# Marks of the chosen cells moved to ScalarE, the low digit's one-hot in one comparison, and new orders, in an audio tower kernel

## The reference, cut to what matters

```
sc0, ix0 = top_k(s0, 16); sc1, ix1 = top_k(s1, 16)      # 64 keys each
cs = sc0[:, None] + sc1[None, :]                         # 16 x 16 cells
ci = ix0[:, None] + ix1[None, :]                         # the expert of a cell
fs, pos = top_k(cs, 16); fi = ci[pos]
w = softmax(fs)
inner = einsum(h, expert_down[fi]); act = gelu(inner)
out = sum over heads and chosen experts of (act * w) @ expert_up[fi]
```

## Time and profile before

| | us |
|---|---|
| median of 3 runs | 1461.08 |
| lowest and highest | 1459.81, 1461.68 |
| profiled execution | 1458.15 |
| its span, first to last instruction | 1456.3 |
| VectorE busy | 1332.5 (91%) |
| TensorE busy | 1219.2 (84%) |
| GpSimd busy | 975.1 (67%) |
| ScalarE busy | 894.5 (61%) |

### The profile page before, as it was taken

How to read it: one execution, slowest core, us unless ns; L and a number is a source line. 1 busy time by engine, 2 the same in 40 slices (tenths; PEclk the granted TensorE clock), 3 DMA queues, 4 the chain that set the end, 5 groups by cost and what they waited for, 6 DMA issues and landing times.

```text
span 1456.3 us, 41234 instructions
## 1 busy us (share of the span) xinstructions
PE 1219.2 (84%) x9633; PEld 711.9 (49%) x9633; DVE 1332.5 (91%) x10235; ACT 894.5 (61%) x4105; POOL 975.1 (67%) x1850
## 2 busy tenths in 40 slices
PE   4788887898888988888887979898898889998873
PEld 2434554644554464545445445554645555463343
DVE  4349999999999999999999999999999999998995
ACT  2566757567576656757675775767567576655532
POOL 4428667686867668586766857577685867667562
PEclk7777687767777676877867786687668777675655
DMA  2000000000000000000000000000000000000000
GB/s 52 12 6 2 3 10 4 4 8 5 9 4 10 3 5 10 5 9 4 11 4 4 10 4 10 5 10 4 5 8 6 4 4 5 3 4 3 5 3 7
DMA packets 22351, 10.49 MB, mean 7 GB/s; under 512 B 13839, under 2 KB 21951, under 8 KB 22080
## 3 DMA queue, kind: packets, MB, share of 16 engines
q1 hardware_dynamic: 21456, 7.30, 2.1%
q10 hardware_dynamic: 624, 0.30, 0.1%
HBM read 4.58 MB, written 3.01 MB: 5 GB/s over the span
## 4 chain that ended last, share of the span: by engine, by line
DVE 35%; PE 28%; issue 15%; POOL 14%; ACT 7%; SPq 1%; POOLq 1%; DVEq 0%; DMA 0%; ACTq 0%
DVE idx L1404 8%; DVE val L1402 5%; DVE oh L1417 4%; DVE scores L1407 4%; DVE cr L1471 4%; PE bankS L1132 3%; PE bankS L1131 3%; PE bankQ L1121 3%; PE bankQ L1120 3%; DVE best L1469 3%; ACT ns_junk L829 3%; PE bankM L1168 3%; PE bankQ L1108 2%; POOL std L561 2%; DVE wl L1436 2%
## 5 line engine op out<-in xcount | busy, mean ns | idle before, releaser
L1404 DVE FIND_INDEX8 idx<-val,scores 124x8 uint16<-124x64 f32 x1536 | 304.8, 217 | 0.0
L1168 PE MATMUL bankM<-wl,oh 128*128 128x16 f16 x5952 | 163.7, 173 | 59.5 <-DVE wl L1436 59.5
L1402 DVE MAX8 val<-scores 124x8 f32<-124x64 f32 x1536 | 211.1, 209 | 2.1 <-ACT scores L836 2.0
L1168 PEld LDWEIGHTS bankM<-wl,oh 128*128 128x128 f16 x5952 | 161.2, 101 | 72.6 <-issue 41.1
L595 POOL TENSOR_TENSOR ce<-idxf 124x128 f32<-124x128 f32 (+4 forms) x240 | 95.4, 429 | 115.9 <-ACT idxf L843 115.8
L829 ACT ACTIVATE ns_junk<-bankQ 124x32 f32<-124x32 f32 x768 | 138.2, 265 | 37.7 <-PE bankQ L1121 37.7
L1417 DVE TENSOR_SCALAR oh<-eh 128x992 f16<-128x992 int16 x384 | 150.4, 457 | 2.3 <-ACT eh L877 2.3
L1407 DVE MATCH_REPLACE8 scores<-val,scores 124x64 f32<-124x64 f32 x768 | 151.7, 208 | 0.0
L569 POOL TENSOR_TENSOR qscale<-nmx,power 124x16 f32<-124x16 f32 x48 | 139.9, 2914 | 0.0
L829 ACT ACTIVATION_READ_ACCUMULATOR ns_junk<-bankQ 124x1 f32 x768 | 138.3, 278 | 0.0
L1132 PE MATMUL bankS<-bias9k,std9T 9*124 9x512 f32 x192 | 132.2, 774 | 0.0
(11 more groups left out here) (188 smaller groups left out, 3185.0 us busy)
## 6 DMA issues: line engine op xcount, KB each, us to landing
x_in<-in_x SPq DMA_DIRECT2D x16, 93.8 KB
x_in<-in_x SPq DMA_DIRECT2D x16, 62.5 KB
out<-o_sb SPq DMA_DIRECT2D x16, 62.0 KB
out<-o_sb SPq DMA_DIRECT2D x16, 61.0 KB
out<-o_sb SPq DMA_DIRECT2D x16, 60.5 KB
x_in<-in_x SPq DMA_DIRECT2D x16, 31.0 KB
conv_w<-in_L_tok_kernel ACTq DMA_DIRECT2D x2, 128.0 KB, 3.0
fwq_in<-in_L_ffn_Wq SPq DMA_DIRECT2D x1, 256.0 KB
```

The source lines that it names most:

```text
L1168: last = e.matmul(coef[:, g, :, :], oh[:, k, g, :, :].rearrange("p v t -> p (v t)"), wl[:, part, k, :, TG * g:TG * (g + 1)], start=k + par ...
L1402: last = v.max(out=v_[:, hd, s, best8], in_=src[:, hd, s, :])
L1404: last = v.max_index(out=i_[:, hd, s, best8], in_max=v_[:, hd, s, best8], in_values=src[:, hd, s, :])
```

## The change

Three things. First, the filler becomes a power of two, `taken` becomes f16, and `mark` leaves VectorE: ScalarE copies `cr` with the scale 4096 / filler, which gives 4096 where the filler stands and rounds to 0 elsewhere. Its semaphore is `marked`. VectorE's first replacement of the next tile waits for it, since it overwrites `cr`. `chosen` counts 10 per tile. Second, a constant tile `lows` holds 0, 1, 2, 3, and `one_low` compares the whole with it in one instruction. Third, the orders of all engines but SyncE are written anew.

```diff
-NEG = -1.0e30
+NEG = -2.0 ** 100
...
-        taken = sb("taken", [NT, H, NC])
+        taken = sb("taken", [NT, H, NC], f16)
...
+        lows = sb("lows", [128, EL, NT], i16)
...
# GpSimd, select
-                pool.wait_ge(chosen, 11 * n + 9)
+                pool.wait_ge(marked, n + 1)
...
# ScalarE
+            def mark(c, t):
+
+                n = c.tile(t)
+                act.wait_ge(chosen, 10 * n + 8)
+                wait(act, weights, 4 * n - 2)
+                a.activation(taken[:, :, :], cr[:, :, :], ACT.Copy, scale=WSCALE / NEG).then_inc(marked, 1)
...
# VectorE
+                for l in range(EL):
+                    v.memset(lows[:, l, :], l)
...
-                for l in range(EL):
-                    last = v.tensor_scalar(ol[:, :, l, :], el[:, :, :], float(l), None, ALU.is_equal)
-                last.then_inc(wl_ready, 1)
+                v.tensor_tensor(ol[:, :, :, :], el[:, :, :].unsqueeze(2).to_broadcast([128, 2, EL, NT]),
+                                lows[:, :, :].unsqueeze(1).to_broadcast([128, 2, EL, NT]), ALU.is_equal).then_inc(wl_ready, 1)
...
+                    if step == 1 and q == 0:
+                        wait(dve, marked, n)
...
-            def mark(c, t):
-
-                n = c.tile(t)
-                wait(dve, weights, 4 * n)
-                dve.wait_ge(chosen, 11 * n + 8)
-                v.tensor_scalar(taken[:, :, :], cr[:, :, :], NEG / 2, WSCALE, ALU.is_lt, ALU.mult).then_inc(chosen, 1)
```

More of the change, by code:

```diff
@@ L292, in build @@
         chosen = sem("chosen")
+        marked = sem("marked")
         weights = sem("weights")
@@ L579, in rank_sums @@
                     pool.wait_ge(ranked, 16 * n + 6)
-                    wait(pool, chosen, 11 * n - 7)
+                    wait(pool, chosen, 10 * n - 6)
                     wait(pool, exp_ready, n)
@@ L649, in body @@
                 do(p1_rstd, c + 2, 0)
+                do(q_scale, c, 2)
+                do(select, c, 1)
+                do(normalise, c, 1)
+                do(rank_sums, c, 2, 0)
+                do(rank_sums, c, 2, 1)
+                do(rank_sums, c, 2, 2)
                 if at(c, -2):
@@ L883, in body @@
             def body(c):
[L884 to L887, removed]
+                do(weight_high, c + -1, 2)
                 do(q_squares, c, 1)
                 do(p1_probs, c + 1, 1)
-                do(weight_high, c + -1, 2)
                 do(p1_attnT, c + 1, 0)
                 do(p1_diag, c + 1, 1)
+                do(q_stdT, c, 1)
                 do(cells_T, c + -1, 2)
                 do(p1_axT, c + 1, 0)
-                do(q_stdT, c, 1)
                 do(p1_probs, c + 1, 2)
+                do(merged_weights, c + -1, 2)
+                do(p1_attnT, c + 1, 1)
                 do(index_floats, c, 0)
-                do(p1_attnT, c + 1, 1)
-                do(merged_weights, c + -1, 2)
                 do(p1_diag, c + 1, 2)
@@ L903, in body @@
                 do(cell_exp, c, 0)
+                do(q_scores, c, 1)
                 do(best_exps, c, 0)
-                do(q_scores, c, 1)
+                do(mark, c, 0)
                 do(p1_axT, c + 1, 1)
@@ L929, in body @@
                     copy_weights()
+                do(q_stdT, c + 1, 0)
+                do(mark, c, 1)
+                do(p1_ln, c + 2, 0)
                 do(cell_exp, c, 1)
-                do(q_stdT, c + 1, 0)
-                do(p1_ln, c + 2, 0)
                 do(q_norms, c + 1, 0)
@@ L938, in body @@
                 do(q_gelu, c + 1, 1)
+                do(cells_T, c, 1)
                 if at(c, -1):
                     q_scores(c + 1, 0)
-                do(cells_T, c, 1)
                 do(q_gelu, c + 1, 2)
+                do(index_floats, c, 2)
                 do(merged_weights, c, 1)
                 do(q_gelu, c + 1, 3)
+                do(cell_exp, c, 2)
                 do(p1_probs, c + 2, 0)
-                do(index_floats, c, 2)
+                do(mark, c, 2)
                 do(best_exps, c, 2)
+                do(p1_diag, c + 2, 0)
+                if not at(c + 1, 0):
+                    do(q_scores, c + 1, 0)
             run(act, start, body, lambda: None)
@@ L1180, in body @@
             def body(c):
+                do(scatter, c + -2, 1)
+                do(p1_scores, c, 2)
                 do(turn_cells, c + -2, 2)
@@ L1587, in body @@
                 do(choose, c, 0, 1)
-                do(choose, c, 0, 2)
                 do(one_high, c + -1, 2, 0)
```

90 lines of the change are left out of this document (41 added, 49 removed).

## The result

The changed kernel takes 1474.54 us (median; 1466.17 to 1488.98) against 1459.81 us of the kernel before (1448.09 to 1465.1), 11 runs each on the same chip: a ratio of 1.012, 95% interval 1.0089 to 1.0152. The execution of 1488.98 us is a slow one and is left out of the ratio; the next is 1485.58. It is slower by 1.2%, where 1.5% faster was forecast, and lies above the range. The profiled execution took 1481.37 us with a span of 1479.6, 23.3 us more than the span before. It is 6.8 us over the median, at a mean granted clock of 0.694 of full speed; the kernel before was profiled at 0.723.

A forecast was written before the change was run, and what follows sets the result against it. VectorE, busy 97.3% of the steady stretch, was taken as the bound. Savings of 13.4 + 11.0 = 24.4 us, 23.4 after head and tail, less 2 for handing over, gave 21.4 off 1461.08: 1439.5 us, range 1428 to 1458.5.

The forecast's parts named there:

- I take 0 for it, bounds -10 and +10: New step orders on the engines: no time won or lost, within 10 us either way.
- Sum. 13.4 + 11.0: VectorE time saved by moving the marks (13.4 us) and by the single low-digit comparison (11.0 us), added to 24.4 us.
- one microsecond less of VectorE work per batch is close to one microsecond less per batch: Steady stretch: VectorE work saved becomes nearly equal time saved, as long as the other engines follow.
- 13 disturbed ones, 1.1 us each: Low-digit one-hot on VectorE: the single comparison gains 1.1 us in each of 13 tiles disturbed by GpSimd's `sq_pairs` and `sq_win`.
- `wl` never over 781 ns: VectorE's two-input product `wl`, sometimes beside GpSimd's work, peaked at 781 ns; evidence against the new comparison being held up.
- The marks leave VectorE: 48 `taken` instructions leave VectorE, 0.28 us each from start to start: 13.4 us of VectorE time go.
- their arrival on ScalarE: 48 mark copies on ScalarE, 27 us, hidden by its free time; handing over to `select` loses 2 us, bounds 0 and 12.
- The slower rival: Tile 0's mark holds `axT` and `attnT` on ScalarE, `res` on VectorE waits; 2.4 us per batch gives 1475 us; chance 0.10.
- The first rival: Another engine, TensorE by its clock or ScalarE, takes up half of the gain: 1450 us; chance 0.13.
- The rival of a comparison held up beside the window sums: New comparison delayed 1.2 us at a time beside `sq_pairs` and `sq_win`, a loss of 4.6 us: 1454.5 us; chance 0.07.
- The signs: Observations set to show the forecast wrong: `ol` above 1 us, `res` waits above 15 us, VectorE under 95%, `oh` above 480 ns.
- the rival at one column per cycle: New low-digit comparison runs as slowly as f32 tensor-tensors, losing 10.8 us: 1458.5 us; chance 0.05.

The follow-up runs named there:

- scores first: Kernel before with marks on ScalarE, which copies tile 1's scores before tile 0's `best_exps` and `mark`: 1447.08 us; with the one comparison too 1464.72 us.
- run 5: Marks with scores first, both halves of tile 2's `oh` moved ahead of `choose` and the low digit: 1442.55 us with four comparisons, 1461.14 with one.
- run 7: Changed kernel with VectorE's `oh` of tile 1 pulled together ahead of the last two steps of `choose`: 1490.19 us, 1.0222 to the kernel before.
- three pairs: Marks with scores first, four comparisons against one: as is 1447.08 and 1464.72 us, window sums cut 1424.48 and 1440.51, tile 2's `oh` moved 1442.55 and 1461.14.
- the fastest kernel: Fastest complete kernel: marks with scores first, four comparisons, tile 2's `oh` moved ahead of `choose` and the low digit: 1442.55 us, 0.9914 to the kernel before.
- run 3: Changed kernel with GpSimd's order of before, 1473.92 us, or TensorE's order of before, 1474.25 us; ratios to the kernel before 1.0103 and 1.0123.
- run 4: Marks with scores first, GpSimd's window sums cut to 8 to 16 columns: 1424.48 us with four comparisons, 1440.51 us with one.

## Why the prediction was wrong

- **"I take 0 for it, bounds -10 and +10": the orders, the term that failed most.** With the marks and four comparisons they cost 1.8% (0.9935 to 1.0112), with the old instructions 1.8% too (1.0183), some 26 us each. I had bounded them by the idle time of VectorE that they could win and, for the loss, by nothing but symmetry. The row that priced a loss was at hand: an `oh` takes from 414 ns to 1178 ns by what GpSimd does beside it. Four of them beside `select` turned out 1.5 us longer, 21 us in 14 batches, while meetings elsewhere shrank: `oh` as a whole is busy 14.5 us more.
- **"Sum. 13.4 + 11.0": terms priced one by one and added. That step failed too.** The orders have no price of their own. On top of both instructions in the orders of before (1.0176) they take 0.6% away, on top of both with the scores first (1.0056) they add 0.6%, on top of the marks with the scores first 1.8%. And neither does VectorE's time: "one microsecond less of VectorE work per batch is close to one microsecond less per batch" did not hold when the new waits came (run 5: 19.1 us less work, 0.2% less time; run 7: less work and more time).
- **"13 disturbed ones, 1.1 us each": wrong in kind.** The term was right by itself: the slots of `ol`, start to next start, sum to 31.4 us in the changed kernel (31.0 forecast) from 42.5. But the time does not go with the instruction; the GpSimd step delays whatever stands there. An undisturbed one takes 0.59 us by starts against 0.55 for four (0.645 forecast), so nothing was left to gain, and the other direction was missing: the one long comparison holds GpSimd, and in the orders of before one comparison in place of four cost 16 to 19 us in three pairs, none of it without tile 0's. In the new orders that loss does not show (+0.1%), nor does any gain. The evidence that two inputs are safe beside GpSimd, `wl` never over 781 ns, was evidence on the old orders alone: in the changed kernel `wl` takes up to 1266 ns.
- **"The marks leave VectorE", 13.4 us, and their arrival on ScalarE, 2 us: right in mechanism, with one wait overlooked.** With scores first VectorE's busy time falls by 12.7 us and the time by 0.65%, 9.5 us. The steps that I named behind the mark (`axT`, `attnT`) were indeed hidden. In the changed kernel `axT` runs at 710.46, right behind a mark that waited 2.45 us, and TensorE asks for it at 712.78. `q_scores`, which the change moved ahead of the mark and which the prediction does not name, was the wait that mattered: behind the mark it costs 27 us of waiting.
- **The slower rival** gave 1475 us and the result is 1474.5. That is luck: it needed 2.4 us a batch at `res`, 38 us in all, with the gain of 24.4 kept, and `res` waits 18.2 us, 14.5 more than before. Its mechanism, `axT` held behind the mark, is not the cause either: the marks with scores first leave that wait at 4.6 us, and the fastest kernel has 17.7. The first rival, that another engine takes up the gain because of TensorE's clock, was the one that the profile came nearest to, but I let it take half of the gain at most; how far it is the cause stays open (behind run 3). The rival of a comparison held up beside the window sums was right that nothing is saved there.
- **The sums.** 1461.08 less 21.4 is 1439.7, not 1439.5, and the rival at one column per cycle leaves out the 2 us for handing over; with them it is 1460.5. Neither changes the outcome.
- **The signs** that I had set: `oh` above 480 ns came (493 ns). `res` above 15 us in the stretch did not (13.3 us), nor did `ol` above 1 us (0.73 in the mean), nor VectorE under 95% busy (96.0%).
- **What is shown and what is open.** Along one path the runs go -0.65% (marks, scores first), +1.8% (new orders), +0.1% (one comparison, within its interval). That they end at +1.2% is no confirmation, since the last run of the path is the changed kernel. That the new orders, met with the marks, lose what the marks win is shown; by which step is not. The meeting of `select` with tile 1's `oh` is seen in the trace, but removing it (run 7) changed waits as well, and no run held the clock apart from the orders.

## What to carry to other kernels

When VectorE is 97% busy, an instruction's duration is partly the price of what GpSimd does at that moment. Price the meeting, not the instruction: making the disturbed instruction shorter moves the disturbance to its neighbour, and only moving one of the two steps (run 5) or shortening the other one (run 4) takes it away. Whether time follows is a second question: it did in run 4 and hardly in run 5. Bound a reordering by the longest such meeting times the number of batches, and list for each step that waits on a queue what stood behind it before and stands there now. One long tensor-tensor in place of several short instructions also takes the gaps away through which the other engine got on, so look at short steps of the critical side chain beside it, as `lnv` here. And a matching total or a matching wait does not confirm a mechanism: remove it and see whether the time follows. Before waits of two profiles are compared, compare their times with their medians and their granted clocks.

## What the runs showed of the hardware

- Both engines hold each other. A three-column GpSimd step took 0.24 us beside four tensor-scalar comparisons of 248 columns and 0.69 us beside one tensor-tensor comparison of 992; a step of 0.85 us took 3.32 us beside eight tensor-scalar comparisons of 992, and four of these took 2.90 us instead of 1.39 beside two GpSimd products of 400 columns.
- Three GpSimd steps of 0.8 to 1.0 us per batch cost VectorE 29.7 us in 16 batches, 1.9 us per batch, by its busy time with and without them; the time of the kernel fell by 22.6 us.
- An int16 to f16 tensor-tensor comparison with two broadcast inputs runs as fast as the f16 product `wl`: 0.68 us undisturbed for 992 columns.
- In executions of one kernel on one chip the time went from 1466.17 us at a mean granted clock of 0.711 to 1485.58 us at 0.685; whether the clock made the time no run shows.
